# A fused two-layer transformer block on one core: the first stage in another order

## The reference

```
x = x + tanh(g_xattn[0]) * L0_attention(layernorm(x), ctx)      # 16 heads of 16; keys and values: context, then own rows
x = x + tanh(g_ffn[0])   * L0_quantised_ffn(layernorm(x))       # 704 wide, silu(gate) * up, rounded to 8 bits
x = x + tanh(g_xattn[1]) * L1_attention(layernorm(x), ctx, ctx) # keys and values: context only
x = x + tanh(g_ffn[1])   * L1_experts(layernorm(x))             # 8 experts, the best 2 of each row
```

```
q, k, v = split(x @ w_attn + b_attn);  kc, vc = split(ctx @ w_ref + b_ref)
w = softmax(masked(q . [kc, k] / 4) - 2 on the context's columns)
out = (w @ [vc, v]) @ w_proj + b_proj
```

## Time and profile before

| | |
|---|---|
| time of 3 runs | 669.93 us median, 668.5 to 672.32 |
| profiled execution | span 664.1 us; it has no time of its own beside the span |
| TensorE busy | 515.1 us, 78% |
| VectorE busy | 429.5 us, 65% |
| ScalarE busy | 297.8 us, 45% |
| GpSimd busy | 162.6 us, 24% |
| mean granted TensorE clock | 0.861 |

### The profile page before, as it was taken

The page is one execution under the profiler, slowest core; times in us unless marked ns, Lnnn a source line. Parts: engine busy times, 40 slices in busy tenths (PEclk is TensorE's granted clock), DMA queues, the critical chain, the costliest instruction groups (busy, mean ns, idle before and its releaser), DMA issues. The chain is left out here.

```text
span 664.1 us, 15475 instructions
## 1 busy us (share of the span) xinstructions
PE 515.1 (78%) x5403; PEld 356.1 (54%) x5403; DVE 429.5 (65%) x921; ACT 297.8 (45%) x482; POOL 162.6 (24%) x191
## 2 busy tenths in 40 slices
PE   2477798998988898737547878998975269999994
PEld 1263365665666667523223545655654258887782
DVE  7365576667686774387754856777569875666662
ACT  6442145556556538203314546676753223333331
POOL 5500022122122211010045410122125044444432
PEclk9989588979999977668659788999976569999997
DMA  9136834444535700000073787789347111222210
GB/s 258 40 120 113 161 82 105 105 115 110 112 99 140 188 5 25 1 1 0 0 154 88 181 155 151 142 165 178 121 158 270 60 40 28 48 40 47 49 19 1
DMA packets 73247, 64.31 MB, mean 97 GB/s; under 512 B 33326, under 2 KB 65750, under 8 KB 73190
## 3 DMA queue, kind: packets, MB, share of 16 engines
q1 hardware_dynamic: 61544, 41.37, 28.3%
q0 software_dynamic: 8224, 21.06, 12.0%
q10 hardware_dynamic: 3424, 1.12, 0.8%
HBM read 48.59 MB, written 15.92 MB: 97 GB/s over the span
## 5 line engine op out<-in xcount | busy, mean ns | idle before, releaser
L467 PEld LDWEIGHTS PS<-QS,KS 112*120 112x120 f16 (+2 forms) x896 | 81.9, 144 | 29.9 <-issue 10.9
L467 PE MATMUL PS<-QS,KS 112*120 112x100 f16 (+2 forms) x896 | 92.8, 229 | 5.1 <-ACT PT L530 3.7
L578 DVE CUSTOM_DVE_ANT_0 PS<-PS,maskv 100x461 f32<-100x461 f32 x128 | 80.5, 647 | 15.2 <-PE PS L436 14.3
L581 DVE TENSOR_REDUCE mx<-PS 100x1 f32<-100x361 f32 x128 | 63.6, 529 | 35.8 <-PE PS L439 34.7
L530 ACT ACTIVATE PT<-PS 120x400 f32<-120x400 f32 (+1 forms) x128 | 63.4, 503 | 45.5 <-PE PS L467 43.1
L530 ACT ACTIVATE PT<-PS,ctxb 120x400 f32<-120x400 f32 (+1 forms) x96 | 57.0, 596 | 52.7 <-PE PS L467 51.9
L436 PE MATMUL PS<-KS,QS 65*100 65x461 f16 x128 | 52.6, 416 | 17.9 <-DVE mx L578 17.3
L795 POOL TENSOR_SCALAR_AFFINE_SELECT PT<-PT 100x400 f32<-100x400 f32 x32 | 17.7, 553 | 187.6 <-ACT PT L530 187.6
L2025 PE MATMUL PS<-aT,WE 128*128 128x128 f16 x960 | 59.4, 224 | 0.0
L2025 PEld LDWEIGHTS PS<-aT,WE 128*128 x960 | 57.0, 101 | 0.0
L2038 PE MATMUL PS<-WE,hidden_high 128*128 x160 | 53.0, 379 | 0.0
(11 more groups left out here) (307 smaller groups left out, 1069.7 us busy)
## 6 DMA issues: line engine op xcount, KB each, us to landing
share<-in_L_ffn_w_dram POOLq DMA_DIRECT2D x13, 1024.0 KB, 9.3
k_scratch<-share SPq DMA_DIRECT2D x32, 180.5 KB, 2.5
KS<-k_scratch SPq DMA_DIRECT2D x32, 180.5 KB, 3.6
KS<-k_scratch SPq DMA_DIRECT2D x64, 90.2 KB, 6.3
QS<-q_scratch SPq DMA_DIRECT2D x64, 50.0 KB, 2.7
v_scratch<-xn SPq DMA_DIRECT2D x8, 385.7 KB
values_staged<-v_scratch SPq DMA_DIRECT2D x8, 385.7 KB
WE<-in_L_ffn_w_dram POOLq DMA_DIRECT2D x2, 1024.0 KB, 8.6
```

What stands on the lines that cost most here:

```text
L467: last = nc.tensor.matmul(bank[0:kn, i * T:(i + 1) * T], KS[p][:, h, k0:k0 + kn], QS[p][:, h, :], start=True, stop=True)
L578: nc.vector.tensor_tensor_reduce(rows, rows, maskv[:, :], 1.0, -BIG, ALU.add, ALU.max, mx[p][:, h:h + 1]).then_inc(s_smf, 1)
L581: nc.vector.tensor_reduce(mx[p][:, h:h + 1], sm_bank[h % 2][0:T, 0:TC], X, ALU.max).then_inc(s_smf, 1)
```

## The change

- `wide_of(n)`: the first ten wide tiles alternate between tiles 0 and 1 (banks 0 to 3) instead of running through all four, so banks 4 to 7 are free for the context's products beside them. TensorE waits for the evacuation of the last but one wide tile where it waited for the fourth last.
- The head rows are written in quarters of four heads: two quarters of stack 0 around the high half of the attention weights, two while own values are made, and the four of stack 1 ahead of the first maxima. `pe_N` now waits for all eight, where the first row waited for both halves.
- Context 0 is turned right behind the input. Its two keys of the first layer go between own queries and own keys; context 1 is turned behind own keys, and its two first keys are made behind own values. The two keys of the second layer follow the second layer's weights, for each context, with four score rows between them.
- The splitting of the reference and projection weights goes ahead of the queries' evacuation on ScalarE and VectorE. The scaling of the bias rows goes behind it.
- The nine small loads go from ScalarE's queue to SP's, behind the load of context 1. SP writes the first context's keys ahead of own keys, and loads context 2 behind the first stack.
- The 16 first score rows go through four banks (0 to 3) and in fours: 4 ahead of the last two keys of context 1, and 4 behind each value product.

The diff, without the places where `wide[n % 4]` became `wide_of(n)` in the helpers:

```diff
@@ -92,6 +92,12 @@
 PS = top.enter_context(nc.psum_tensor("PS", [P, 8, 512], F32))
 wide = [PS[:, 2 * w:2 * w + 2, :].rearrange("p a n -> p (a n)") for w in range(4)]
+NW = 10
+def wide_of(n):
+    return wide[n % 2 if n < NW else n % 4]
 sm_bank = [PS[:, 0, :], PS[:, 1, :]]
...
@@ -370,7 +376,8 @@
...
-SM0 = (0, 5, 10, 16)
+SM0 = (4, 8, 12, 16)
+NSB = 4
...
@@ -438,6 +445,15 @@
...
+def pe_SM0(pe, h):
+    if h % HM == 0:
+        pe.wait_ge(s_ks[0][h // HM], 16 * 6)
+    if h >= NSB:
+        pe.wait_ge(s_smf, h - NSB + 1)
+    nc.tensor.matmul(PS[0:T, h % NSB, 0:S0], QS[0][0:KROWS + 1, h, :], KS[0][0:KROWS + 1, h, :],
+                     start=True, stop=True).then_inc(s_smd, 1)
 def pe_N(pe, j, o, smn, freed):
...
@@ -580,6 +596,14 @@
     else:
         nc.vector.tensor_reduce(mx[p][:, h:h + 1], sm_bank[h % 2][0:T, 0:TC], X, ALU.max).then_inc(s_smf, 1)
+def dve_max0(dve, h):
+    dve.wait_ge(s_smd, h + 1)
+    dve.sem_inc(s_rb, 1)
+    rows = PS[0:T, h % NSB, 0:S0]
+    nc.vector.tensor_tensor_reduce(rows, rows, maskv[:, :], 1.0, -BIG,
+                                   ALU.add, ALU.max, mx[0][:, h:h + 1]).then_inc(s_smf, 1)
 def dve_norm(dve, j, o, bsum):
...
@@ -669,21 +693,28 @@
...
+        for dst, src in (
+                (gts[:, 0:2], g_xattn.partition_broadcast(P)), (gts[:, 2:4], g_ffn.partition_broadcast(P)),
...
+            sp.dma_start(dst, src).then_inc(s_small, 16)
...
+        sp.wait_ge(s_mf, 4)
+        sp_keys_out(sp, 0, 0, 0)
...
-        sp.wait_ge(s_mf, 2)
-        sp_ctx(sp, 0, 2)
-        sp.wait_ge(s_mf, 4)
-        sp_keys_out(sp, 0, 0, 0)
...
-        sp.wait_ge(s_mf, 10)
+        sp_ctx(sp, 0, 2)
+        sp.wait_ge(s_mf, 8)
...
@@ -817,47 +848,53 @@
...
+        def head_rows(p, q):
+            hs = slice(q * HG, (q + 1) * HG)
+            nc.scalar.activation(KS[p][IROW:KX, hs, :], delta[:, hs].unsqueeze(2).to_broadcast([H, HG, S0]),
+                                 ACT.Copy).then_inc(s_kr, 1)
         act.wait_ge(s_dl, 1)
-        for p in range(2):
-            nc.scalar.activation(KS[p][IROW:KX, :, :], delta[:, :].unsqueeze(2).to_broadcast([H, H, S0]), ACT.Copy
-                                 ).then_inc(s_kr, 1)
+        head_rows(0, 0)
         act.wait_ge(s_wr[0], 16)
         nc.scalar.activation(wah[:, :, :], r_attn, ACT.Copy, scale=WS).then_inc(s_wh8, 1)
+        head_rows(0, 1)
         for kc in range(KC):
             wide_hi(act, kc, xTh[:, kc, :])
-        for dst, src in (
-                (gts[:, 0:2], g_xattn.partition_broadcast(P)), (gts[:, 2:4], g_ffn.partition_broadcast(P)),
...
-            act.dma_start(dst, src).then_inc(s_small, 16)
+        for kc in range(KC):
+            act_hi_T(act, 0, 0, kc, kc)
+        act.wait_ge(s_wr[1], 32)
+        nc.scalar.activation(wrh[:, :, :], r_ref[:, :, 0:D], ACT.Copy, scale=WS)
+        nc.scalar.activation(wvh[:, :, 0, :], r_ref[:, :, D:2 * D], ACT.Copy, scale=WS)
+        nc.scalar.activation(wph[:, 0, :, :], r_proj, ACT.Copy, scale=WS).then_inc(s_wh8, 1)
...
+        for k in range(2):
+            act_hi_K(act, 0, 0, k, 2 + k)
         for mb in range(KC):
             wide_hi(act, 4 + mb, skh[:, mb, :], bcol[:, 1, mb:mb + 1])
-        act.wait_ge(s_wr[1], 32)
-        act.wait_ge(s_small, 16 * 9)
-        nc.scalar.activation(wrh[:, :, :], r_ref[:, :, 0:D], ACT.Copy, scale=WS)
-        nc.scalar.activation(wvh[:, :, 0, :], r_ref[:, :, D:2 * D], ACT.Copy, scale=WS)
-        nc.scalar.activation(wph[:, 0, :, :], r_proj, ACT.Copy, scale=WS).then_inc(s_wh8, 1)
-        nc.scalar.activation(tg[:, :], gts[:, :], ACT.Tanh)
-        nc.scalar.activation(clipt[:, :], clips[:, :], ACT.Tanh, scale=0.5).then_inc(s_tanh, 1)
+        for kc in range(KC):
+            act_hi_T(act, 0, 1, kc, 4 + kc)
+        head_rows(0, 2)
+        head_rows(0, 3)
+        for k in range(2):
+            act_hi_K(act, 0, 1, k, 6 + k)
...
-                last = nc.scalar.activation(dst, wide[n % 4][:, 512 * i:512 * i + 512].rearrange(
+                last = nc.scalar.activation(dst, wide_of(n)[:, 512 * i:512 * i + 512].rearrange(
...
-            for kc in range(KC):
-                act_hi_T(act, 0, o, kc, 6 * o + kc)
-            for k in range(4):
-                act_hi_K(act, 0, o, k, 6 * o + 2 + k)
+            for k in range(2, 4):
+                act_hi_K(act, 0, o, k, 6 + 2 * o + k)
+        act.wait_ge(s_small, 16 * 9)
+        nc.scalar.activation(tg[:, :], gts[:, :], ACT.Tanh)
+        nc.scalar.activation(clipt[:, :], clips[:, :], ACT.Tanh, scale=0.5).then_inc(s_tanh, 1)
+        for q in range(H // HG):
+            head_rows(1, q)
         act_max_rows(act, 0, 0, 0, 0)
         act_max_rows(act, 0, 0, 1, 0)
@@ -910,46 +947,54 @@
...
+        for kc in range(KC):
+            pe_T(pe, 0, 0, kc, kc)
...
+        pe.wait_ge(s_split, 2)
+        for k in range(2):
+            pe_K(pe, 0, 0, k, 2 + k, 1)
         for mb in range(KC):
-            pe.wait_ge(s_wf, 4 + mb - 3)
+            pe.wait_ge(s_wf, 4 + mb - 1)
             project_T(pe, 4 + mb, wah, wal, KC + mb)
+        for kc in range(KC):
+            pe_T(pe, 0, 1, kc, 4 + kc)
         for n in range(2):
-            pe.wait_ge(s_wf, 6 + n - 3)
+            pe.wait_ge(s_wf, 6 + n - 1)
...
-                    last = split3(pe, wide[(6 + n) % 4][0:T, i * D:(i + 1) * D],
+                    last = split3(pe, wide_of(6 + n)[0:T, i * D:(i + 1) * D],
...
+        for k in range(2):
+            pe_K(pe, 0, 1, k, 6 + k, 5, True)
         pe.wait_ge(s_wr[2], 64)
         for n in range(2):
-            pe.wait_ge(s_wf, 8 + n - 3)
+            pe.wait_ge(s_wf, 8 + n - 1)
...
-                        last = nc.tensor.transpose(wide[(8 + n) % 4][:, o0:o0 + P],
+                        last = nc.tensor.transpose(wide_of(8 + n)[:, o0:o0 + P],
                                                    r_l1[2 * n + i][:, ob, kc * P:(kc + 1) * P], ident[:, :])
             last.then_inc(s_wd, 1)
-        pe.wait_ge(s_split, 2)
         pe.wait_ge(s_wf, 10)
-        for o in range(2):
-            n0 = 6 * o
-            for kc in range(KC):
-                pe_T(pe, 0, o, kc, n0 + kc)
-            for k in range(4):
-                pe_K(pe, 0, o, k, n0 + 2 + k, n0 + 1)
-        pe.wait_ge(s_kr, 2)
+        for k in range(2, 4):
+            pe_K(pe, 0, 0, k, 6 + k, 1)
         pe.wait_ge(s_kz, 1)
+        for h in range(SM0[0]):
+            pe_SM0(pe, h)
+        for k in range(2, 4):
+            pe_K(pe, 0, 1, k, 8 + k, 5)
...
-                pe_SM(pe, 0, 0, h, 0, 0)
+                pe_SM0(pe, h)
+        pe.wait_ge(s_kr, 2 * H // HG)
         pe_N(pe, 0, 0, 0, 15)
         def turning(k):
@@ -1019,23 +1064,15 @@
...
-        dve.wait_ge(s_bias, 16 * 8)
-        nc.vector.tensor_scalar(brow[:, :, :], brow[:, :, :], WS, None, ALU.mult)
-        nc.vector.tensor_scalar(bcol[:, :, :], bcol[:, :, :], WS, None, ALU.mult).then_inc(s_biasp, 1)
...
-        dve.wait_ge(s_biasp, 1)
-        for mb in range(KC):
-            wide_lo(dve, 2 + mb, qh[:, mb, :], ql[:, mb, :], bcol[:, 0, mb:mb + 1])
-        for mb in range(KC):
-            wide_lo(dve, 4 + mb, skh[:, mb, :], skl[:, mb, :], bcol[:, 1, mb:mb + 1])
-        for p in range(2):
-            nc.vector.memset(V1s[p][:, :, :, DH:VW], WS)
-        nc.vector.memset(Vs[:, :, :, DH:VW], WS)
+        for kc in range(KC):
+            dve_lo_T(dve, 0, 0, kc, kc, kc)
+        dve.wait_ge(s_bias, 16 * 8)
+        nc.vector.tensor_scalar(bcol[:, :, :], bcol[:, :, :], WS, None, ALU.mult).then_inc(s_biasp, 1)
...
@@ -1043,38 +1080,56 @@
...
+        nc.vector.tensor_scalar(brow[:, :, :], brow[:, :, :], WS, None, ALU.mult).then_inc(s_biasp, 1)
+        dve.wait_ge(s_biasp, 1)
+        for mb in range(KC):
+            wide_lo(dve, 2 + mb, qh[:, mb, :], ql[:, mb, :], bcol[:, 0, mb:mb + 1])
+        for k in range(2):
+            dve_lo_K(dve, 0, 0, k, 2 + k, 2 + k)
+        for mb in range(KC):
+            wide_lo(dve, 4 + mb, skh[:, mb, :], skl[:, mb, :], bcol[:, 1, mb:mb + 1])
+        for kc in range(KC):
+            dve_lo_T(dve, 0, 1, kc, 4 + kc, 4 + kc)
+        for p in range(2):
+            nc.vector.memset(V1s[p][:, :, :, DH:VW], WS)
+        nc.vector.memset(Vs[:, :, :, DH:VW], WS)
+        dve.wait_ge(s_biasp, 2)
...
-                    wide[(6 + n) % 4][0:T, i * D:(i + 1) * D].rearrange("p (h d) -> p h d", h=H),
+                    wide_of(6 + n)[0:T, i * D:(i + 1) * D].rearrange("p (h d) -> p h d", h=H),
                     brow[0:T, 0, :].rearrange("p (h d) -> p h d", h=H), ALU.add)
             last.then_inc(s_wf, 1)
+        for k in range(2):
+            dve_lo_K(dve, 0, 1, k, 6 + k, 6 + k)
...
-                    out=lo, in0=wide[n % 4][:, 512 * i:512 * i + 512].rearrange("p (k n) -> p k n", k=KC),
+                    out=lo, in0=wide_of(n)[:, 512 * i:512 * i + 512].rearrange("p (k n) -> p k n", k=KC),
                     scalar=WS, in1=hi, op0=ALU.mult, op1=ALU.subtract)
             last.then_inc(s_wf, 1)
```

(50 more changed lines are left out.)

5 lines of the change are left out of this document (removed).

## The result

The changed kernel took 646.0 us in the median of its first 4 runs (638.89 to 652.34) against 669.21 before. The ratio is 0.963, 95% interval 0.956 to 0.970. Two later sets of 6 runs gave 645.9 and 645.2, beside 17 and 11 runs of the kernel before with medians of 664.9 and 664.85: ratios 0.970 (0.963 to 0.976) and 0.970 (0.965 to 0.975). The change is worth some 20 us, 3%. Ratios and their intervals leave out executions that took over 1.5% longer than the fastest of the same kernel; the medians hold all.

A forecast was written before the change was run, and what follows sets the result against it. Outside the first stage TensorE's queue sets the time; within it TensorE mostly waits. Moving the maxima's transpose from 79.86 to 61.7 gains 18 us: span 664.1 - 18 = 646, median 652, own range 648 to 657.

The forecast's parts named there:

- the clock stays up: Rival, chance 0.07: TensorE at 2.4 GHz throughout, transpose of the maxima at 58.3, round 0 gains 2.7 us, time 646.
- the mark: Transpose of the first row maxima, ending the first stage; forecast to move from 79.86 to 61.7 us.
- The walk: First stage followed step by step along four queues: first product 16.75, last wide tile freed 40.9, transpose of the maxima 61.7.
- Maxima 0.6 apart: Sign in the first stage's tail: VectorE's row maxima come 0.6 us apart where four are queued.
- Head rows done ahead of the transpose: Sign in the first stage: the last head-row piece ends before the maxima's transpose, by 4 us.
- The stack: First stack's loads start at 33.8 instead of 55.17, after own keys written by 31.5; halves land at 41 and 45.
- a mix of both, 60.4, and add 1.3: First stage's tail: transpose between 58.3 all warm and 63.2 all cold, plus 1.3 us for longer hand-overs, giving 61.7.
- 664.1 - 18 = 646, and 652 as a median: Whole kernel: profiled span less the 18 us gain, with the median 5.8 us above the span as before.
- Constant rows in pieces ... 8.2 us earlier: Start of the first stage: head rows in quarters let TensorE begin its products at 16.75, not 24.93.
- Nothing gained: Moving nine small loads from ScalarE's queue to SP's in the first stage is worth zero.
- Transfers in the waits' place: Rival, chance 0.10: first stack's halves land at 48 and 58, transpose at 67 to 68, gain 12, time 658.
- Slower: Rival, chance 0.04: behind the first stage more rounds run at half clock; with 60 us more of it, 676.

The follow-up runs named there:

- pieces alone: The kernel before with only the constant head rows written in quarters and spread between other work; 659.6 us, ratio 0.992.
- the earlier keys: The changed kernel with the last keys of context 0 waiting for wide tile 8 only, the score rows for tile 9; 642.2 us, ratio 0.968.
- the gap filled: The changed kernel with 12 unused matmuls ahead of the last keys of context 0; 638.5 and 641.7 us in two sets.

## Why the prediction was right and wrong

The time was forecast at 652, range from 646.0 up, and came out at its lower edge or just below: 646.0, 645.9 and 645.2. The direction and the mechanism were right; two terms of the sum were not, the tail of the stage and, more, the level to which its gain was applied. The time is also the 646 of the rival "the clock stays up" (chance 0.07), but not by its mechanism: the mark came at 59.5, between its 58.3 and the forecast's 61.7, and round 0 did not gain its 2.7 us (24.7 long, 24.6 before). That rival's own sum, 669.9 - 21.5 - 2.7, is 645.7, not 646.

- *The walk.* First product 16.75, measured 16.76. TensorE without a gap to 38.1: 38.0. Last tile freed at 40.9: 40.85. Maxima 0.6 apart: yes. Head rows done ahead of the transpose: yes, at 54.5 (47.89 + 6.62). Rounds behind unchanged: yes. Part of the closeness is luck. By the walk's own prices the steps from 16.75 on add up to 38.5, not 38.1 (5.88 for the queries, 4.06 for the keys); it came out because the first product took 3.71 and not 3.85, and the turning of context 1 0.62 and not 0.9. And the first rows, given as 41.9 to 43.7, are 42.8 to 44.5 by those prices (two keys of 0.94 or 1.78 behind 40.9); they came at 44.28.
- *The stack.* The first stack's loads were forecast at 33.8 and were issued at 36.22. The last own keys' write was issued by 32.17 (forecast 31.5), and its landing took 4.05 us, not the 2.3 of before. It cost nothing here, as the first row came at 44.28.
- *The step that was off in the stage* is the last term of the tail, "a mix of both, 60.4, and add 1.3": 61.7 against 59.5, 2.2 us. The clock was low for 3.4 us behind the gap, not for 6.8 as before, and full in the sparse tail, so the mix was 0.9 too high and the added 1.3 had nothing to stand for. I read the low clock of before at 66.2 as the price of sparse rows. The new tail is sparse too (TensorE busy 6.11 of 9.50, before 1.89 of 3.50 ahead of the fall) and kept full clock to its end, and with pieces alone the old tail itself was low for only some 5 us. What made the one fall and not the other stays open.
- *The step that was off in the total* is "664.1 - 18 = 646, and 652 as a median". I took the 5.8 us between the profile's span and the median of three as fixed. A run's time is about 1.7 us above its own span (645.21 and 643.5), so the profiled execution took about 665.8 by estimate, and the three runs happened to lie high: 50 later ones have a median of 664.9. From there 18 us lead to 647, and the 20.3 measured to 644.6. This term is 4 to 5 of the 6 us missed, the tail 2.
- *Attribution.* "Constant rows in pieces ... 8.2 us earlier" gave the pieces what in part was the bias scaling's: 5.2 and 3.0. The sum was right since both are in the change; with the head rows whole, the later scaling gave nothing.
- *"Nothing gained" by the small loads' queue* was wrong in the new order: 2.9 us at the last keys of context 0, 1.4 of it left at the mark. I asked what they cost where they had stood, not where they would stand. The Trainium skill's rule (DMA: Bandwidth & Descriptors, "Issuing engines are not separate DMA queues") says that another queue saves the issue time alone; the trace agrees: this was that issue time, 3.69 us of ScalarE.
- *Transfers in the waits' place:* the stack was in by 44.28, no row waited. It is the next limit: with the earlier keys the first row waited for it until 42.64, against the 41 of the walk and the 48 of this rival.
- *Slower:* the stage's gain is there in full, and no round behind it grew.

## What to carry to other kernels

A start-up stage where queues hand work to each other can be walked row by row. Here that came within 3 us at every step, and within 0.1 us at some, of which part was luck; a term added for caution only took it further off. Ask of each moved instruction what stands behind it in its new place: issues that cost nothing under a long operation cost their full length in front of a short one. Take the level of the time from many runs, each against its own span, before a gain of a few us is taken off it. And when an edit's worth is read from one mark in one profile, compare the clock ahead of the mark in both: with the small loads it hid half of the cost, and with two banks it made half of it.

## What the runs showed of the hardware

- Two simple VectorE operations (fp32 in and out, one source) took 0.16 and 0.55 us alone, 2.08 and 3.00 beside GpSimd's memsets of 3.2 us, and ended with a memset (19.49 and 19.47) or 0.4 us behind one (23.02 and 22.61). The Trainium skill (SBUF — State Buffer, "Who interferes with whom") says that VectorE in a two-port mode and GpSimd block each other for a whole instruction. The trace agrees in these ends; that the two operations ran in that mode no row shows.
- After 21 us of unbroken matmuls, a TensorE gap of 2.82 us was followed by a stretch at 1.2 GHz in all three profiles of the changed kernel; with the gap filled or cut to 1.63 us it was not. But with the small loads on ScalarE's queue the same 2.82 us, 14 us behind a shorter pause, were followed by 2.4 GHz (granted 1.00 from 43.8 to 48.0), and with two banks 1.2 GHz came behind a gap of 1.65 us and two rows (0.51 from 46.6 to 50.1). The length of the gap does not decide it alone; what else does stays open.
- The same second-layer attention took 99.0 to 108.1 us from one profile to another by nothing that was changed in it, and 105.2 to 108.1 in three profiles of one kernel. A gain of 4 us ahead of it is inside that.
